# Projecting q two tiles ahead in the windowed-attention layers of a six-layer network

## The chip, the cores and the metric

The kernel runs on one core of one Trainium2 chip. The metric is the time of one execution on the device in microseconds (us). The profile covers one execution of the kernel before; the names of the engines in it are PE (TensorE matmul), PEld (TensorE weight load), DVE (VectorE), ACT (ScalarE), POOL (GpSimd) and SP (SyncE, which issues the DMAs).

## The reference

A sequence of 2048 tokens with 128 features goes through two blocks of pre-normalised attention, a feed-forward part with four-bit quantisation between them, and then six layers of another network. Only these six layers are touched by the change. Each layer is, with 16 heads of 64 elements and windows of 32 tokens:

```python
for i in range(DEPTH):                                # DEPTH = 6
    x = attn_layer(shift_tokens(x), ...) + x
    x = ffn_layer(shift_tokens(x), ...) + x

def attn_layer(x, Wqkv, qs, ksc, Wo):
    q, k, v = jnp.split(x @ Wqkv, 3, -1)              # 3 x 1024 columns, 16 heads
    q = l2norm(q) * qs;  k = l2norm(k) * ksc
    q = q * cos * scale + rotate_half(q) * sin * scale
    k = k * cos / scale + rotate_half(k) * sin / scale
    out = local_attention(q, k, v)                    # softmax over this window and the one before
    return out @ Wo
```

The feed-forward part is a layer norm, two products, a gelu gate and a third product.

## The kernel before, in words

The function `layers` writes, by hand, one instruction list for each engine. The only order within an engine is the one written, and engines meet only through counting semaphores: an instruction that waits holds up all that stands behind it on its engine. Layers 0 to 4 run in a hardware loop, the sixth layer is written out once more behind it. Within a layer the 2048 tokens are 16 tiles of 128 (`NT` = 16). The names below carry (l, T): layer and tile.

For each tile the steps are, with the engine that does them:

- `project(T, i, b)` (PE, L1023): the product of the tile with half of the columns of q (i = 0), k (i = 1) or v (i = 2); b is the half. q and k both go to PSUM banks 0 and 1, so each half waits until the `normalise` of the previous one has read the bank. v goes to the banks of the scores and waits for `subtract` of the tile before. Each half is two matmul rows in the trace.
- `squares` (ACT, L1231), `sum_squares` (DVE, L1376 twice and L1378), `inverse_norms` (ACT, L1237 and L1239), `normalise` (DVE, L1389, two halves): the L2 norm of q and of k.
- `cosines` (DVE, L1397) and `rotate` (POOL, L966 and L967 into the single buffer `sine`) make the two rotary products. For q, POOL adds them too (L973). For k, `add_rotated` on DVE does (L1405).
- `turn(T, r)` (PE, L1037): four transposes; r = 0 and 1 are q, 2 and 3 are k. `store_qk` (ACT, L1252 to L1259) copies the result out.
- `scores` (PE, L1048 and L1055), `maxima` and `subtract` (DVE, L1411 and L1417), `exponentials` (ACT, L1267), `sums` (DVE, L1424 and L1426), `normalise_weights` (POOL, L990): the softmax.
- `turn_weights` (PE, L1070), `place_low` (ACT, L1273) and `place_high` (DVE, L1433): the weights, transposed, each half f in two parts. `values` (PE, L1088), `store_o` (ACT, L1281), `out_project` (PE, L1100) and `residual` (DVE, L1440) finish a tile.

The steps of several tiles are interleaved: in iteration T of `attend`, before the change, each engine works on the norms of q and k of tile T+1, the scores of T, the values of T-1 and the output projection of T-2. SP moves a copy of v, shifted by a window, with two DMAs for each tile. After the 16 tiles comes `forward`, the feed-forward part.

## Time and profile before

| | |
|---|---|
| median of 3 runs | 3716.92 us (3702.21 to 3720.24) |
| the profiled execution: its time, its span | 3709.67 us, 3707.6 us |
| mean granted TensorE clock | 0.926 of full speed |
| busy: PE, PEld, DVE, ACT, POOL | 2984.7, 1623.0, 2847.8, 2071.5, 1071.0 us |
| first and last product of the layers (L1023) | 1647.7 us, 3634.0 us |
| DMA | 100.96 MB, mean 27 GB/s |

The span is the time from the first to the last instruction in the trace. A busy time sums the time in which an engine works on an instruction; waiting is not in it. The clock is a share of TensorE's full 2.4 GHz. The six layers fill the span from 1614 us on.

### The profile page before, as it was taken

What the parts mean: (1) busy time and instruction counts of PE and PEld (TensorE: products, weight loads), DVE (VectorE), ACT (ScalarE), POOL (GpSimd) and SP (SyncE); (2) the same over time, 40 slices, a digit from 0 to 9 for tenths busy, and PEclk for the clock granted to TensorE, in tenths of its full rate; (3) what the DMA queues carried; (4) which work ended last, traced back from release to release, by engine and by line L of the source; (5) the groups of instructions that cost most, each with busy time, mean ns of one, the idle gap of its engine ahead of it and who ended that gap; (6) DMA issues with size and microseconds to landing.
All of it is one profiled execution on the core that took longest, in us unless ns stands there. A gap on an engine that the chain in (4) does not pass through costs nothing. (4 is left out here: it accounts for less than half of the span.)

```text
span 3707.6 us, 73298 instructions
## 1 busy us (share of the span) xinstructions
PE 2984.7 (81%) x28669; PEld 1623.0 (44%) x28669; DVE 2847.8 (77%) x4196; ACT 2071.5 (56%) x3147; POOL 1071.0 (29%) x614
## 2 busy tenths in 40 slices
PE   4999999944369999957887888788878878887888
PEld 1233333313223333325663565466455635654664
DVE  5999999957626778737886887788678868877885
ACT  2577777752213455636664666566556646665664
POOL 0000000000000000035553554455355535544561
PEclk7899999977657898969999999999999999999999
DMA  3000000000120000011111111011111111110110
GB/s 114 29 1 2 2 2 2 1 7 0 64 66 1 2 1 1 1 50 35 34 46 28 30 30 48 25 34 30 36 36 30 45 33 30 30 48 24 36 30 23
DMA packets 57088, 100.96 MB, mean 27 GB/s; under 512 B 20182, under 2 KB 38548, under 8 KB 55316
## 3 DMA queue, kind: packets, MB, share of 16 engines
q1 hardware_dynamic: 56740, 96.18, 8.8%
q8 instruction: 236, 3.87, 0.4%
q14 instruction: 112, 0.92, 0.1%
HBM read 38.22 MB, written 7.34 MB: 12 GB/s over the span
## 5 line engine op out<-in xcount | busy, mean ns | idle before, releaser
L471 DVE TENSOR_REDUCE a_part<-ps 128x1 f32<-128x512 f32 (+3 forms) x1664 | 993.4, 653 | 204.5 <-PE ps L343 190.4
L452 ACT ACTIVATE a_Pb<-ps 128x1024 f32<-128x1024 f32 (+3 forms) x832 | 767.8, 975 | 475.3 <-PE ps L417 472.2
L1023 PE MATMUL ps<-l_w_qkv,l_XS 128*128 128x512 f32 x1152 | 577.5, 624 | 217.5 <-DVE l_weights L1417 158.1
L343 PE MATMUL ps<-a_KS,a_QS 48*128 48x512 bf16 (+3 forms) x1664 | 503.4, 398 | 66.7 <-DMA a_QS<-pieces 30.5
L966 POOL TENSOR_TENSOR l_sine<-l_qn,l_tab 128x512 f32<-128x512 f32 x192 | 341.1, 1777 | 641.9 <-DVE l_qn L1389 641.4
L393 PE MATMUL ps<-a_Pb,V 128*32 128x256 f32 (+2 forms) x6144 | 441.2, 402 | 0.9 <-ACT a_Pb L452 0.9
L1376 DVE TENSOR_REDUCE l_bounded<-l_square 128x8 f32<-128x512 f32 x384 | 254.6, 684 | 217.9 <-ACT l_square L1231 211.9
L1023 PEld LDWEIGHTS ps<-l_w_qkv,l_XS 128*128 128x128 f32 x1152 | 203.7, 197 | 393.4 <-DVE l_weights L1417 170.6
L417 PE MATMUL ps<-a_QS,a_KS 50*128 50x512 bf16 (+3 forms) x1664 | 323.2, 379 | 17.3 <-ACT a_Pb L452 14.9
L1389 DVE TENSOR_TENSOR l_qn<-ps,l_norm 128x512 f32<-128x512 f32 x384 | 246.7, 684 | 86.7 <-ACT l_norm L1239 86.7
L1037 PE MATMUL ps<-ident,l_hat 128*128 128x128 f32 x1536 | 217.8, 276 | 115.2 <-DVE l_hat L1405 115.2
L343 PEld LDWEIGHTS ps<-a_KS,a_QS 48*128 48x128 bf16 x1664 | 125.3, 94 | 422.4 <-DVE a_part L471 322.7
L1037 PEld LDWEIGHTS ps<-ident,l_hat 128*128 128x128 f32 x1536 | 178.8, 141 | 230.6 <-issue 196.1
L990 POOL TENSOR_TENSOR l_weights<-l_weights,l_rcp 128x1024 f32<-128x1024 f32 x96 | 188.9, 1968 | 282.5 <-DVE l_rcp L1426 282.5
L1397 DVE TENSOR_TENSOR l_cosine<-l_qn,l_tab 128x1024 f32<-128x1024 f32 x192 | 252.0, 1312 | 9.4 <-POOL l_tab L981 5.3
L1231 ACT ACTIVATE l_square<-ps 128x512 f32<-128x512 f32 x384 | 228.4, 596 | 42.9 <-PE ps L1023 35.0
L967 POOL TENSOR_TENSOR l_sine<-l_qn,l_tab 128x512 f32<-128x512 f32 x192 | 247.7, 1290 | 0.0
L973 POOL TENSOR_TENSOR l_hat<-l_cosine,l_sine 128x1024 f32<-128x1024 f32 x96 | 226.8, 2363 | 20.5 <-POOL l_sine L967 19.3
L1055 PEld LDWEIGHTS ps<-l_kT,l_qT 128*64 128x64 f32 x6144 | 195.8, 138 | 82.8 <-issue 82.8
L393 PEld LDWEIGHTS ps<-a_Pb,V 128*32 128x32 f32 x6144 | 158.9, 110 | 167.1 <-issue 87.6
L631 POOL MEMSET f_w<- 128x1120 f32 x1 | 1.0, 1032 | 777.7 <-POOLq L284 777.7
L1055 PE MATMUL ps<-l_kT,l_qT 128*64 128x64 f32 x6144 | 222.4, 226 | 0.0
(182 smaller groups left out, 4554.8 us busy)
## 6 DMA issues: line engine op xcount, KB each, us to landing
l_V_earlier<-l_V SPq DMA_DIRECT2D x96, 384.0 KB, 3.5
l_V_earlier<-l_V SPq DMA_DIRECT2D x96, 128.0 KB, 3.4
l_w_qkv<-in_L_ffn_Wqkv_dram SPq DMA_DIRECT2D x6, 1536.0 KB, 8.1
pieces<-a_piece SPq DMA_DIRECT2D x12, 512.0 KB, 2.6
a_QS<-pieces SPq DMA_DIRECT2D x96, 64.0 KB
a_KS<-pieces SPq DMA_DIRECT2D x24, 192.0 KB
l_w_o<-in_L_ffn_Wo_dram SPq DMA_DIRECT2D x6, 512.0 KB, 4.0
a_cos<-in_c_cos_dram SPq DMA_DIRECT2D x2, 1024.0 KB, 5.4
```

The costliest lines, as they stand in the source:

```text
L343: mm = e.matmul(bank[:, 0:width], QS[rows, c, pair, qt * P:(qt + 1) * P], KS[rows, pair, b * CH:b * CH + width], start=not masked, stop=Tr ...
L393: mm = e.matmul(O[32 * h:32 * h + 32, a:b], t.V[:, kt, w:w + 32], Pb[:, n % 2, h, a:b], start=(kt == 0), stop=(kt == tiles_of(c) - 1), ski ...
L417: mm = e.matmul(ps[:, h, a:CH], KS[rows, 2 * g + p, kt * P:(kt + 1) * P], QS[rows, c, 2 * g + p, a:CH], start=not diagonal, stop=True, ski ...
L452: e.activation(Pb[:, n % 2, 2 * p:2 * p + 2, a:CH], ps[:, 2 * p:2 * p + 2, a:CH], ACT.Exp)\
L471: e.tensor_reduce(part[:, u % 2, column(h, qt), b:b + 1], bank[:, 0:width], AX.X, ALU.max)\
L966: e.tensor_tensor(sine[:, :, 0:ROT], swap[:, :, ROT:LD], table[:, :, 0:ROT], ALU.mult).then_inc(s.rotated, 1)
L967: e.tensor_tensor(sine[:, :, ROT:LD], swap[:, :, 0:ROT], table[:, :, ROT:LD], ALU.mult).then_inc(s.rotated, 1)
L1023: e.matmul(ps[:, (V_BANK[T] if i == 2 else 0) + b, :], XS[:, T * P:(T + 1) * P], w_qkv[:, at:at + CH], start=True, stop=True).then_inc(s.a ...
L1037: tr = e.transpose(ps[:, TURN_BANK[r], j * P:(j + 1) * P], hat[:, i, at:at + P], t.ident[:, :])
L1055: mm = e.matmul(ps[half:half + LD, bank, at:at + LD], qT[:, T % 2, j, w, :, :], kT[:, T % 2, j, WIN * w:WIN * (w + 2)], start=False, stop= ...
L1376: e.tensor_reduce(bounded[:, heads, 0], square[:, heads, :], AX.X, ALU.add).then_inc(s.total, 1)
L1397: e.tensor_tensor(cosine[:, i, :, :], qn[:, i, :, :], tab[:, 2 * i, T, :].unsqueeze(1).to_broadcast([P, LH, LD]), ALU.mult).then_inc(s.cos ...
```

## The change

Order and placing are changed in the layers' attention part; no arithmetic is.

- q is projected two tiles ahead. In iteration T, `project(T + 2, 0, .)` stands behind `values(T - 1)` and ahead of the projection of v, where q of T+1 was projected between the turns of T, behind v. `squares`, `sum_squares`, `inverse_norms`, `normalise` and `cosines` of q move with it on ACT and DVE, `rotate` of q on POOL is renamed but keeps its place. At T = 0 the q of tile 1 is done by itself.
- k of T+1 is projected ahead of `turn_weights(T - 1)`, where it was behind it.
- The turns 0 and 1 of q follow each other, and `out_project` stands between turn 1 and turn 2 as before.
- `add_rotated` moves from behind the sums to ahead of them, and one tile earlier: in iteration T it adds k of T+1.
- ACT: the k squares stand ahead of `place_low`, and `inverse_norms` of k between its two halves. DVE: `place_high`'s halves stand ahead of and behind `normalise` of k.
- v's products count on a semaphore of their own (`v_ready`), and the clearing of 32 old semaphores gets a block of its own ahead of the layers' first one.

```diff
--- before.py
+++ after.py
@@ -860,6 +860,12 @@
...
+        with nc.Block() as block:
+            @block.sync
+            def _(e):
+                for signal in t.spent:
+                    e.sem_clear(signal)
...
-                    for signal in t.spent:
-                        e.sem_clear(signal)
@@ -909,7 +913,7 @@
                 def load_weights(l):
-                    e.wait_ge(s.a_ready, START + l * (6 * NT))
+                    e.wait_ge(s.v_ready, START + l * (2 * NT))
                     e.dma_start(w_qkv[:, :], a["L1_ffn_Wqkv"][l]).then_inc(s.w_qkv, 16)
@@ -991,11 +995,13 @@
                 def attend(l):
+                    rotate(l, 1, 0)
                     for T in range(NT):
                         if T + 1 < NT:
-                            for i in range(2):
-                                rotate(l, T + 1, i)
+                            rotate(l, T + 1, 1)
                         normalise_weights(l, T)
+                        if T + 2 < NT:
+                            rotate(l, T + 2, 0)
 
...
+                e.sem_inc(s.v_ready, START)
@@ -1021,7 +1028,7 @@
                     e.matmul(ps[:, (V_BANK[T] if i == 2 else 0) + b, :], XS[:, T * P:(T + 1) * P], w_qkv[:, at:at + CH],
-                             start=True, stop=True).then_inc(s.a_ready, 1)
+                             start=True, stop=True).then_inc(s.v_ready if i == 2 else s.a_ready, 1)
 
@@ -1118,27 +1125,29 @@
                         ahead = T + 1 < NT
-                        if ahead:
-                            project(l, T + 1, 0, 0)
+                        if T == 0:
+                            project(l, 1, 0, 0)
+                            project(l, 1, 0, 1)
                         turn(l, T, 0)
-                        if ahead:
-                            project(l, T + 1, 0, 1)
                         turn(l, T, 1)
                         if T >= 2:
                             out_project(l, T - 2)
                         turn(l, T, 2)
                         turn(l, T, 3)
+                        if ahead:
+                            project(l, T + 1, 1, 0)
+                            project(l, T + 1, 1, 1)
                         if T:
                             turn_weights(l, T - 1, 0)
                             turn_weights(l, T - 1, 1)
-                        if ahead:
-                            project(l, T + 1, 1, 0)
-                            project(l, T + 1, 1, 1)
                         scores(l, T, 0)
                         scores(l, T, 1)
                         if T:
                             values(l, T - 1, 0)
                             values(l, T - 1, 1)
+                        if T + 2 < NT:
+                            project(l, T + 2, 0, 0)
+                            project(l, T + 2, 0, 1)
                         if ahead:
@@ -1225,7 +1234,7 @@
                     n = (l * NT + T) * 2 + i
-                    e.wait_ge(s.a_ready, START + (l * NT + T) * 6 + 2 * i + b + 1)
+                    e.wait_ge(s.a_ready, START + (l * NT + T) * 4 + 2 * i + b + 1)
                     if b == 0:
@@ -1239,7 +1248,7 @@
                 def store_values(l, T):
-                    e.wait_ge(s.a_ready, START + (l * NT + T) * 6 + 6)
+                    e.wait_ge(s.v_ready, START + (l * NT + T) * 2 + 2)
                     e.copy(V[:, T % 3, :], flat2(ps[:, V_BANK[T]:V_BANK[T] + 2, :])).then_inc(s.v_done, 1)
@@ -1295,27 +1304,30 @@
                         ahead = T + 1 < NT
-                        if ahead:
-                            squares(l, T + 1, 0, 0)
-                        store_qk(l, T, 0)
-                        if ahead:
-                            squares(l, T + 1, 0, 1)
-                        store_qk(l, T, 1)
-                        if ahead:
-                            inverse_norms(l, T + 1, 0)
-                        store_qk(l, T, 2)
-                        store_qk(l, T, 3)
-                        if T:
-                            place_low(l, T - 1, 0)
-                            place_low(l, T - 1, 1)
+                        if T == 0:
+                            squares(l, 1, 0, 0)
+                            squares(l, 1, 0, 1)
+                            inverse_norms(l, 1, 0)
+                        for r in range(4):
+                            store_qk(l, T, r)
                         if ahead:
                             squares(l, T + 1, 1, 0)
                             squares(l, T + 1, 1, 1)
+                        if T:
+                            place_low(l, T - 1, 0)
+                        if ahead:
                             inverse_norms(l, T + 1, 1)
+                        if T:
+                            place_low(l, T - 1, 1)
                         if T:
                             store_o(l, T - 1, 0)
                             store_o(l, T - 1, 1)
+                        if T + 2 < NT:
+                            squares(l, T + 2, 0, 0)
+                            squares(l, T + 2, 0, 1)
                         exponentials(l, T)
+                        if T + 2 < NT:
+                            inverse_norms(l, T + 2, 0)
                         if ahead:
@@ -1456,32 +1468,35 @@
                         ahead = T + 1 < NT
-                        if T:
-                            sums(l, T - 1)
-                        if ahead:
-                            sum_squares(l, T + 1, 0)
-                        if T:
-                            add_rotated(l, T)
-                        if ahead:
-                            normalise(l, T + 1, 0)
-                            cosines(l, T + 1, 0)
+                        if T == 0:
+                            sum_squares(l, 1, 0)
+                            normalise(l, 1, 0)
+                            cosines(l, 1, 0)
                         if T >= 2:
                             residual(l, T - 2)
                         if not ahead:
                             e.wait_ge(s.added, START + l * NT + NT - 2)
                             for c in range(NC - 1):
                                 shift(c, s.xs)
+                        if ahead:
+                            sum_squares(l, T + 1, 1)
                         if T:
                             place_high(l, T - 1, 0)
+                        if ahead:
+                            normalise(l, T + 1, 1)
+                        if T:
                             place_high(l, T - 1, 1)
-                        if ahead:
-                            sum_squares(l, T + 1, 1)
-                            normalise(l, T + 1, 1)
                         maxima(l, T)
                         subtract(l, T)
+                        if T + 2 < NT:
+                            sum_squares(l, T + 2, 0)
                         if ahead:
                             cosines(l, T + 1, 1)
-                    sums(l, NT - 1)
+                            add_rotated(l, T + 1)
+                        sums(l, T)
+                        if T + 2 < NT:
+                            normalise(l, T + 2, 0)
+                            cosines(l, T + 2, 0)
                     residual(l, NT - 2)
```

VectorE, from the maxima of one tile on (inside the loop over the layers; `l_bounded` and `l_norm` are sum_squares, `l_qn` normalise, `l_hat` add_rotated, `l_total` and `l_rcp` sums, `X` the residual). Before:

```order
L1411 TENSOR_REDUCE l_nmax<-ps 128x16
L1417 TENSOR_TENSOR l_weights<-ps,l_nmax 128x1024
L1397 TENSOR_TENSOR l_cosine<-l_qn,l_tab 128x1024
L1424 TENSOR_REDUCE l_total<-l_weights 128x16
L1426 RECIPROCAL l_rcp<-l_total 128x16
L1376 TENSOR_REDUCE l_bounded<-l_square 128x8
L1378 TENSOR_REDUCE l_norm<-l_bounded 128x16
L1405 TENSOR_TENSOR l_hat<-l_cosine,l_sine 128x1024
L1389 TENSOR_TENSOR l_qn<-ps,l_norm 128x512 x2
```

And now:

```order
L1423 TENSOR_REDUCE l_nmax<-ps 128x16
L1429 TENSOR_TENSOR l_weights<-ps,l_nmax 128x1024
L1388 TENSOR_REDUCE l_bounded<-l_square 128x8
L1390 TENSOR_REDUCE l_norm<-l_bounded 128x16
L1409 TENSOR_TENSOR l_cosine<-l_qn,l_tab 128x1024
L1417 TENSOR_TENSOR l_hat<-l_cosine,l_sine 128x1024
L1436 TENSOR_REDUCE l_total<-l_weights 128x16
L1438 RECIPROCAL l_rcp<-l_total 128x16
L1401 TENSOR_TENSOR l_qn<-ps,l_norm 128x512 x2
```

The norms of q (now of T+2) come ahead of k's cosines and addition, and the sums behind both; in both lists q's cosines (not shown) follow the last row.

TensorE, from the last values product of a tile to the output projection (`l_hat` are the turns, `l_oT` the output projection). Before:

```order
L1088 MATMUL ps<-l_wT,l_V 64x2x32 x2
L1023 MATMUL ps<-l_w_qkv,l_XS 128x512 x2
L1019 ISA
L1023 MATMUL ps<-l_w_qkv,l_XS 128x512
L1037 MATMUL ps<-ident,l_hat 128x128 x4
L1100 MATMUL ps<-l_oT,l_w_o 128x128 x8
```

And now:

```order
L1095 MATMUL ps<-l_wT,l_V 64x2x32 x2
L1026 ISA
L1030 MATMUL ps<-l_w_qkv,l_XS 128x512 x4
L1044 MATMUL ps<-ident,l_hat 128x128 x4
L1107 MATMUL ps<-l_oT,l_w_o 128x128 x8
```

The four products in a row are q of T+2 and then v of T+1; before, v stood first and q's two halves stood around the first turn.

## Rows read from the trace of the kernel before

**Rows 1.** Busy time by stretch: us, each engine's busy time, granted clock, DMA share.
```profile
2026.81:2045.92 19.11, 13.57 (x140) 8.81 (x142) 14.42 (x21) 10.16 (x19) 10.17 (x6) 0.91 0.23 56
2045.92:2274.84 228.92, 190.39 (x2378) 138.07 (x2376) 188.92 (x261) 146.28 (x274) 132.67 (x78) 1.00 0.11 31
```

**Rows 2.** VectorE's timeline, one tile: start, us, operation, idle before it and releaser.
```profile
1757.46 1.22 DVE L1411 TENSOR_REDUCE l_nmax<-ps 128x16 f32<-128x1024 f32 x1
1758.71 1.23 DVE L1417 TENSOR_TENSOR l_weights<-ps,l_nmax 128x1024 f32<-128x1024 f32 x1
1759.85 1.42 DVE L1397 TENSOR_TENSOR l_cosine<-l_qn,l_tab 128x1024 f32<-128x1024 f32 x1
1761.19 1.21 DVE L1424 TENSOR_REDUCE l_total<-l_weights 128x16 f32<-128x1024 f32 x1
1762.43 0.25 DVE L1426 RECIPROCAL l_rcp<-l_total 128x16 f32<-128x16 f32 x1
1763.59 0.69 DVE L1376 TENSOR_REDUCE l_bounded<-l_square 128x8 f32<-128x512 f32 x1 [0.91 <-ACT l_square L1231]
1765.27 0.69 DVE L1376 TENSOR_REDUCE l_bounded<-l_square 128x8 f32<-128x512 f32 x1 [0.99 <-ACT l_square L1231]
1765.99 0.19 DVE L1378 TENSOR_REDUCE l_norm<-l_bounded 128x16 f32<-128x32 f32 x1
1766.29 1.23 DVE L1405 TENSOR_TENSOR l_hat<-l_cosine,l_sine 128x1024 f32<-128x1024 f32 x1
1767.44 1.28 DVE L1389 TENSOR_TENSOR l_qn<-ps,l_norm 128x512 f32<-128x512 f32 x2
1768.75 1.23 DVE L1397 TENSOR_TENSOR l_cosine<-l_qn,l_tab 128x1024 f32<-128x1024 f32 x1
1769.89 0.28 DVE L1440 TENSOR_TENSOR X<-X,ps 128x128 f32<-128x128 f32 x1
1770.21 1.30 DVE L1433 COPY l_wT<-ps 64x512 f32<-64x512 f32 x2
1771.54 1.28 DVE L1376 TENSOR_REDUCE l_bounded<-l_square 128x8 f32<-128x512 f32 x2
...
1773.87 1.29 DVE L1389 TENSOR_TENSOR l_qn<-ps,l_norm 128x512 f32<-128x512 f32 x2 [0.82 <-ACT l_norm L1239]
1775.07 1.22 DVE L1411 TENSOR_REDUCE l_nmax<-ps 128x16 f32<-128x1024 f32 x1
```

**Rows 3.** TensorE's timeline in the same tile.
```profile
1759.99 2.84 PE L1023 MATMUL ps<-l_w_qkv,l_XS 128*128 128x512 f32 x6 [1.67 <-DVE l_weights L1417]
...
1767.65 1.09 PE L1037 MATMUL ps<-ident,l_hat 128*128 128x128 f32 x8 [1.30 <-DVE l_hat L1405]
...
1769.48 1.88 PE L1023 MATMUL ps<-l_w_qkv,l_XS 128*128 128x512 f32 x4
1771.20 0.38 PE L1048 MATMUL ps<-l_mask_c,identb 128*128 128x512 bf16 x1
...
1772.59 0.39 PE L1048 MATMUL ps<-l_mask_c,identb 128*128 128x512 bf16 x1
```

**Rows 4.** ScalarE's timeline in the same tile.
```profile
1759.97 1.06 ACT L1267 ACTIVATE l_weights<-l_weights 128x1024 f32<-128x1024 f32 x1 [1.02 <-DVE l_weights L1417]
...
1762.01 1.01 ACT L1243 COPY l_V<-ps 128x1024 f32<-128x1024 f32 x1 [0.98 <-PE ps L1023]
...
1762.96 0.60 ACT L1231 ACTIVATE l_square<-ps 128x512 f32<-128x512 f32 x1
```

**Rows 5.** GpSimd's timeline in the same tile.
```profile
1762.77 1.90 POOL L990 TENSOR_TENSOR l_weights<-l_weights,l_rcp 128x1024 f32<-128x1024 f32 x1 [2.58 <-DVE l_rcp L1426]
...
1768.88 2.22 POOL L966 TENSOR_TENSOR l_sine<-l_qn,l_tab 128x512 f32<-128x512 f32 x1 [4.22 <-DVE l_qn L1389]
```

**Rows 6.** Timeline at the first layer's start, GpSimd.
```profile
1660.35 1.25 POOL L966 TENSOR_TENSOR l_sine<-l_qn,l_tab 128x512 f32<-128x512 f32 x1
1661.56 2.24 POOL L967 TENSOR_TENSOR l_sine<-l_qn,l_tab 128x512 f32<-128x512 f32 x1
```

**Rows 7.** Timeline at the same moment, VectorE.
```profile
1660.38 2.30 DVE L1397 TENSOR_TENSOR l_cosine<-l_qn,l_tab 128x1024 f32<-128x1024 f32 x1 [5.33 <-POOL l_tab L981]
```

**Rows 8.** TensorE's timeline at the start of the second layer.
```profile
2019.43 3.78 PE L1023 MATMUL ps<-l_w_qkv,l_XS 128*128 128x512 f32 x4 [3.59 <-DVE l_qn L1389]
```

**Rows 9.** VectorE's timeline where the layers' first block begins.
```profile
1614.79 2.29 DVE L38 TENSOR_REDUCE stat<-x 128x16 f32<-128x2048 f32 x1 [0.38 <-PEq L284]
```

More of the change, by code:

```diff
@@ L815, in layers @@
     with ExitStack() as ctx:
-        s = semaphores(ctx, nc, "l_", "w_qkv w_tab w_o w_mlp xs tab a_ready square total root qn cosine v_done rotated "
+        s = semaphores(ctx, nc, "l_", "w_qkv w_tab w_o w_mlp xs tab a_ready v_ready square total root qn cosine v_done rotated "
                        "t_ready t_free s_ready nmax sub exp_done sums rcp normed p_ready low high earlier_even earlier_odd "
```

## The prediction

> **What bounds the kernel now.** I read the busy time by stretch first. In thirteen consecutive tiles of the second layer (from one `maxima` to the fourteenth) the clock is full, and VectorE is busy for 188.92 and TensorE for 190.39 of 228.92 us [rows 1]. A tile takes 228.92 / 13 = 17.61 us, and neither engine is full: two engines near 14.6 us each wait for each other. So the timeline of one tile is what counts, VectorE's first. It shows three waits: 0.91 and 0.99 us for the squares of q and 0.82 us for the inverse norms of k, 2.72 us in all [rows 2]. The other 14.9 us are work, from start to start.
>
> Why are q's squares late? On TensorE v's products wait for `subtract` (1.67 us idle), and q's stand behind v's in the queue [rows 3]. The v copy runs on ScalarE at 1762.01 and the first square only at 1762.96 [rows 4]; the second stands behind a store of turned q. So the chain is subtract, v, q, squares, sum_squares, then k's addition, for which TensorE idles another 1.30 us [rows 3]. It is a loop through both engines, once per tile.
>
> **The change part by part.** No instruction is added to a tile or removed. I lay out one tile anew, with t = 0 at the start of `maxima(T)`, service times from start to start and the latencies of the rows.
>
> Service times on VectorE [rows 2]: maxima 1.25, subtract 1.14, sums 1.24, one half of sum_squares 0.72, bound 0.30, add_rotated 1.15, normalise 1.31 (1.20 where a step without dependence follows), cosines 1.14, residual 0.32, one half of place_high 0.67. Cosines of k take 1.34 now; 0.2 of that is the port wait below. TensorE: half a projection 0.86 (k's two halves start at 1769.48, the mask product at 1771.20), q's or k's turns and turn_weights about 0.9 each, one half of the scores 1.40 [rows 3]. One half of values is 0.93: scores end at 1773.99, that is 1756.38 a tile earlier, and the modelled end of values is 1759.99 - 1.67 = 1758.32. Latencies: TensorE to ScalarE 0.30 (v's four rows end at 61.71, the copy starts at 62.01), ScalarE to VectorE 0.03 to 0.14, VectorE to TensorE 0.12.
>
> *q two tiles ahead.* `place_high` of the second half ends at t = 0, values' second half takes 0.1 to 1.03, q's halves end at 1.89 and 2.75, its squares at 2.79 and 3.65. VectorE has finished maxima and subtract at 2.39, so it waits 0.43, and 0.14 before the second half. Two waits of 1.90 become 0.57. v's products (2.75 to 4.47) no longer wait: subtract ended at 2.5. What is behind them now, turns of q and the output projection, runs to 7.2.
>
> *Addition ahead of the sums.* VectorE goes on: bound from 4.40, k's cosines 4.70, add_rotated 5.84, sums 6.98, reciprocal 8.22, normalise q 8.50. The exponentials (1.06 [rows 4]) stand behind q's squares on ScalarE and end at 4.7, so the sums find them. k's turns start at 7.2, without a wait, where 1.30 stood. GpSimd makes k's sines right after `normalise` of k, by about 3, long before 5.84.
>
> *k ahead of turn_weights.* TensorE now has a wait here: k's first half needs q's first half read, at 9.3, and the turns end at 8.1. This idle 1.2 us has turn_weights, scores and values queued behind it. k's products end at 11.02, turn_weights at 11.9, scores at 14.7. VectorE needs the scores only at 16.3, so this costs nothing; its cover is 1.4 us.
>
> *The port.* The sums are later, so `normalise_weights` on GpSimd (1.90 [rows 5]) runs from 8.56 to 10.46, and q's cosines are ready at 9.81. The trace shows what happens when GpSimd and a VectorE instruction with two inputs from SBUF meet: at 1660.38 cosines took 2.30 instead of 1.23, waiting for the end of L966, and L967, issued meanwhile, took 2.24 instead of about 1.25, waiting for the cosines [rows 6, 7]. A 2.22 us sine behind q's cosines is the same on the other side [rows 5]. They exclude each other for a whole instruction. So q's cosines start at 10.46: 0.65 us of new waiting; between 0 (no overlap) and 1.9 (the whole instruction) I take what the layout gives. In return k's cosines meet nobody, and the 0.2 goes.
>
> *The rest of the tile.* Residual 11.60, k's sums of squares 11.92 (squares ready at 11.1 and 11.9), bound 13.36, first half of place_high 13.58, which covers most of the former 0.82 wait; inverse norms are ready at 14.38 (0.13 idle), normalise k to 15.58, second half to 16.27, `maxima(T+1)` at 16.28. ScalarE's longer block is the v copy (5.3 to 6.3), then the stores; the turn in bank 2 waits for the first store until 7.55, just before it is due.
>
> Sum per tile: 17.61 - 1.33 (q's squares) - 0.69 (inverse norms) + 0.65 (port) - 0.2 + about 0.25 of dispatch and seams = 16.3. The gain is 1.31 us, with 13 such intervals in each of 6 layers: 78 x 1.31 = 102 us. The sixth layer is not in the loop; I take the same gain there.
>
> *First interval of a layer*: 19.11 us [rows 1]. Laid out in the same way, without values and place_high, it gives 15.5, so 6 x 3.6 = 22 us. *Last interval*: residual and shifts of X are also behind the later `normalise_weights`; the shifts are SBUF copies and wait for the port. About +0.4, or 2 us in all. *Head of a layer*: at T = 0 all stores stand behind q's inverse norms on ScalarE, which costs, but k's products no longer start 3.59 us idle and at the low clock (3.78 us for four rows against 1.88 [rows 8, 3]). I get 2.2 us less before the first `maxima`; bounds are +3 (the stores come last) and -4; 6 x 2 = 12 us. *The extra block*: the boundary before the layers cost VectorE 0.38 us [rows 9]; one more of those and 32 clears that nothing hides any longer: between 0.4 and 5, I take 3 us.
>
> Total: 102 + 22 - 2 + 12 - 3 = 131 us off the profiled execution's 3709.7. The median of the runs lies 7 us above it, so 3717 - 131, rounded to **3585 us**.
>
> **The rivals.** A measurement of this kernel can tell about 0.5%, 19 us, from no change.
>
> 1. *The seams are smaller or the port collision misses.* If q's cosines come just before or after normalise_weights, a tile takes 15.65; 78 x 0.65 = 51 us more: 3534. For it: the collision depends on an overlap of 0.65 us. Against: normalise q depends on nothing that could move it by that much.
> 2. *A second small wait remains.* The layout has narrow places: the turn in bank 2 (slack 0.1), the squares of k (0.0), ScalarE's queue before the stores. One of them late by 0.7 us per tile: 16.95, or 55 us less gained: 3640.
> 3. *Slower: GpSimd keeps the port.* Behind normalise_weights, GpSimd has q's two sines ready at 9.94. If its queue went on ahead of the waiting cosines, they would start at 10.46 + 2 x 1.26 = 12.98. That is 2.5 us per tile, on the path of everything that follows: 18.8 us per tile, +1.2 x 78 = 94, less 29 of the other terms: 3782. It decides from 1.3 us of extra wait on. The one meeting in the trace in which GpSimd had its next instruction ready speaks against it: the cosines came after one instruction, and L967 waited [rows 6, 7]. The Trainium skill (SBUF - State Buffer, "Who interferes with whom") says that whoever issues first has the pair of ports for its whole instruction; by that, too, the cosines, issued before the sines, would go first, and the sum would stay at 3585.
> 4. *No gain: the loop closes elsewhere.* The slack of 1.4 us before the scores may be eaten, if k's addition or q's normalise moves by more than that; then the tile is bound by TensorE (14.65 us of work and 1.2 idle, plus new waits) near 17.6, and only the ends of the layers gain: about 3690 to 3715.
>
> That the change does not do what it says can be left out: the orders of both engines show it.
>
> **How the numbers follow.** The forecast itself (3560 to 3615) has 0.60, rival 1 has 0.14, rival 2 has 0.14, rival 3 has 0.06, rival 4 has 0.06, two thirds of it within 0.5%. So faster 0.90, same 0.04, slower 0.06. The range takes the forecast with rivals 1 and 2 at their own times: 3530 to 3645.
>
> **What the profile would show.** Right: `maxima` every 16.3 us; two waits for squares of q under 0.5 us each; no idle on TensorE before v's products or k's turns, but 1.2 us before k's products; q's cosines at about 1.75 us and k's at 1.23; normalise_weights still 1.90. Rival 1: cosines 1.23 both. Rival 2: a wait on VectorE above 0.5 us for squares, or on TensorE for a store. Rival 3: q's cosines above 3 us. Rival 4: VectorE waiting for TensorE's scores before `maxima`. I would be wrong altogether if the tile stayed at 17.6 with the waits moved.

## The result and the profile after

The change makes the kernel faster: 3596.97 us, the median of 4 runs (3591.6 to 3605.64), against 3714.53 us for the kernel before on the same chip (4 runs, 3702.21 to 3720.24). The ratio is 0.969, with a 95% interval of 0.9657 to 0.9723. The profiled execution has a span of 3591.1 us, 116.5 less than before, and took 3592.9 us.

The stretches of the second layer first, from the first `maxima` to the second, and the thirteen tiles that follow (columns as in [rows 1]):

```profile
2009.39:2024.52 15.13, 11.97 (x134) 7.58 (x132) 14.63 (x20) 10.49 (x20) 9.50 (x6) 1.00 0.28 71
2024.52:2235.34 210.82, 193.00 (x2366) 140.90 (x2366) 195.33 (x261) 147.01 (x274) 132.83 (x79) 1.00 0.12 34
```

A tile takes 210.82 / 13 = 16.22 us where it took 17.61 [rows 1] (16.20 in twelve of thirteen intervals); VectorE is busy for 93% of it (83% before), TensorE for 92%, at the full clock in both. The time came out of waiting. VectorE's timeline of one tile, from one `maxima` to the next, answers to [rows 2]:

```profile
2137.95 1.23 DVE L1423 TENSOR_REDUCE l_nmax<-ps 128x16 f32<-128x1024 f32 x1
2139.21 1.22 DVE L1429 TENSOR_TENSOR l_weights<-ps,l_nmax 128x1024 f32<-128x1024 f32 x1
2141.03 1.45 DVE L1388 TENSOR_REDUCE l_bounded<-l_square 128x8 f32<-128x512 f32 x2 [0.59 <-ACT l_square L1240]
2142.52 0.19 DVE L1390 TENSOR_REDUCE l_norm<-l_bounded 128x16 f32<-128x32 f32 x1
2142.62 1.22 DVE L1409 TENSOR_TENSOR l_cosine<-l_qn,l_tab 128x1024 f32<-128x1024 f32 x1
2143.97 1.23 DVE L1417 TENSOR_TENSOR l_hat<-l_cosine,l_sine 128x1024 f32<-128x1024 f32 x1
2145.12 1.21 DVE L1436 TENSOR_REDUCE l_total<-l_weights 128x16 f32<-128x1024 f32 x1
2146.36 0.25 DVE L1438 RECIPROCAL l_rcp<-l_total 128x16 f32<-128x16 f32 x1
2146.53 1.24 DVE L1401 TENSOR_TENSOR l_qn<-ps,l_norm 128x512 f32<-128x512 f32 x2
2147.81 1.87 DVE L1409 TENSOR_TENSOR l_cosine<-l_qn,l_tab 128x1024 f32<-128x1024 f32 x1
2149.60 0.28 DVE L1452 TENSOR_TENSOR X<-X,ps 128x128 f32<-128x128 f32 x1
2149.80 1.27 DVE L1388 TENSOR_REDUCE l_bounded<-l_square 128x8 f32<-128x512 f32 x2
2151.10 0.19 DVE L1390 TENSOR_REDUCE l_norm<-l_bounded 128x16 f32<-128x32 f32 x1
2151.32 0.69 DVE L1445 COPY l_wT<-ps 64x512 f32<-64x512 f32 x1
2152.11 1.29 DVE L1401 TENSOR_TENSOR l_qn<-ps,l_norm 128x512 f32<-128x512 f32 x2
2153.43 0.69 DVE L1445 COPY l_wT<-ps 64x512 f32<-64x512 f32 x1
2154.16 1.23 DVE L1423 TENSOR_REDUCE l_nmax<-ps 128x16 f32<-128x1024 f32 x1
```

Of the three waits for other engines one is left as such, 0.59 us for q's squares (0.91 and 0.99 before); the second half of the squares is in the 1.45 us of the merged row, where two reductions without a wait take 1.27 (2149.80). Of the 0.82 us for k's inverse norms 0.10 is left (`place_high` ends at 2152.01, `normalise` starts at 2152.11); the first half of `place_high` covers the rest. New is the length of q's cosines: 1.87 us at 2147.81, where 1.23 stood.

TensorE in the same tile, to be read against [rows 3]:

```profile
2139.15 3.70 PE L1030 MATMUL ps<-l_w_qkv,l_XS 128*128 128x512 f32 x8
2142.68 1.04 PE L1044 MATMUL ps<-ident,l_hat 128*128 128x128 f32 x8
2143.56 1.95 PE L1107 MATMUL ps<-l_oT,l_w_o 128*128 128x128 f32 x16
2145.34 1.07 PE L1044 MATMUL ps<-ident,l_hat 128*128 128x128 f32 x8
2147.23 1.98 PE L1030 MATMUL ps<-l_w_qkv,l_XS 128*128 128x512 f32 x4 [0.82 <-DVE l_qn L1401]
2149.05 1.04 PE L1077 MATMUL ps<-ident,l_weights 128*128 128x128 f32 x8
```

q's and v's eight rows follow each other without a wait, and so do k's turns (2145.34). The one idle time in these rows is 0.82 us before k's products, for q's `normalise`. GpSimd shows the other side of the long cosines, against [rows 5]:

```profile
2146.70 1.90 POOL L994 TENSOR_TENSOR l_weights<-l_weights,l_rcp 128x1024 f32<-128x1024 f32 x1 [5.67 <-DVE l_rcp L1438]
2148.55 2.26 POOL L970 TENSOR_TENSOR l_sine<-l_qn,l_tab 128x512 f32<-128x512 f32 x1
```

`normalise_weights` runs to 2148.60, the cosines issued at 2147.81 end at 2149.68, 1.08 after that, and the sine issued at 2148.55 takes 2.26 us instead of 1.27.

Where the 116.5 us of span went, by the starts of `maxima` (96 in each trace, six layers):

| stretch | before | after | difference |
|---|---|---|---|
| up to the second attention stage's last division (stages not changed) | 1609.54 | 1614.13 | +4.6 |
| from there to the first `maxima` | 74.29 | 74.31 | 0.0 |
| first to second `maxima` of a layer, 6 of them | 115.94 | 90.69 | -25.3 |
| second to fifteenth, 78 intervals | 1369.11 | 1263.23 | -105.9 |
| fifteenth to sixteenth, 6 | 73.03 | 76.99 | +4.0 |
| sixteenth to the next layer's first, 5 | 400.05 | 406.43 | +6.4 |
| last `maxima` to the end | 65.64 | 65.36 | -0.3 |

### The profile page after: what moved, and what is told of

It reads as the page before. It is cut to its first block and busy times, and to the rows that moved or that the text cites. A ratio compares the mean times of both kernels' runs of the same rounds, so it can differ in the third digit from the quotient of the medians.

```text
span 3591.1 us, 72940 instructions
## 1 busy us (share of the span) xinstructions
PE 3005.4 (84%) x28669; PEld 1639.0 (46%) x28669; DVE 2894.9 (81%) x4196; ACT 2076.7 (58%) x3147; POOL 1061.8 (30%) x614
## 5 line engine op out<-in xcount | busy, mean ns | idle before, releaser
L1030 PE MATMUL ps<-l_w_qkv,l_XS 128*128 128x512 f32 x1152 | 565.4, 625 | 127.9 <-DVE l_qn L1401 86.8
L1409 DVE TENSOR_TENSOR l_cosine<-l_qn,l_tab 128x1024 f32<-128x1024 f32 x192 | 292.3, 1523 | 9.6 <-POOL l_tab L985 5.5
L1290 ACT COPY l_oT<-ps 128x512 f32<-128x512 f32 x192 | 112.3, 585 | 226.8 <-PE ps L1095 226.8
L1095 PE MATMUL ps<-l_wT,l_V_earlier 128*64 128x64 f32 x3072 | 193.2, 224 | 46.6 <-DVE l_wT L1445 44.2
L1044 PE MATMUL ps<-ident,l_hat 128*128 128x128 f32 x1536 | 204.7, 277 | 23.3 <-ACT l_qT L1262 17.1
```

Of the source, the lines that this page charges most:

```text
L1030: e.matmul(ps[:, (V_BANK[T] if i == 2 else 0) + b, :], XS[:, T * P:(T + 1) * P], w_qkv[:, at:at + CH], start=True, stop=True).then_inc(s.v ...
L1409: e.tensor_tensor(cosine[:, i, :, :], qn[:, i, :, :], tab[:, 2 * i, T, :].unsqueeze(1).to_broadcast([P, LH, LD]), ALU.mult).then_inc(s.cos ...
```

## The experiments

All are edits of the changed kernel. The medians of two of them come from different chips unless said, and in these traces the unchanged stages ahead of the layers end up to 33 us apart. So I judge by the tile, the distance of two `maxima` in layers 0 to 4 (the value that most of the 65 have), and give the median beside it.

### q behind v again

```diff
+                        if ahead:
+                            project(l, T + 1, 2, 0)
+                            project(l, T + 1, 2, 1)
                         if T + 2 < NT:
                             project(l, T + 2, 0, 0)
                             project(l, T + 2, 0, 1)
-                        if ahead:
-                            project(l, T + 1, 2, 0)
-                            project(l, T + 1, 2, 1)
```

> The changed kernel with v's products put back ahead of q's on TensorE; all else stays as changed. Theory: the gain comes from q's squares no longer standing behind v, which waits for subtract. With v first, the products of q start 1.7 us after subtract instead of right behind values; the squares come about 3.1 us later, and VectorE, with k's cosines, the addition and the sums now queued behind q's sums of squares, has nothing to cover it. One tile takes 19.0 to 19.4 us instead of 16.20, the wait for q's squares is above 3 us, the time is about 3597 + 78 x 3.0 = 3830 us (3790 to 3860). Rival (the gain is in the order on VectorE): the tile stays below 17 us and the time below 3660.

Measured: 3955.84 us (3951.21 to 3966.6), ratio to the kernel before 1.065 (1.0614 to 1.0687); a tile takes 20.46 us. So this order carries the gain, and without it the rest of the change is a loss. But the tile is 1.1 to 1.5 us longer than I expected. VectorE's wait for q's squares, and TensorE in that tile:

```profile
2223.12 1.45 DVE L1388 TENSOR_REDUCE l_bounded<-l_square 128x8 f32<-128x512 f32 x2 [3.65 <-ACT l_square L1240]
```

```profile
2219.52 3.70 PE L1030 MATMUL ps<-l_w_qkv,l_XS 128*128 128x512 f32 x8 [1.27 <-DVE l_weights L1429]
...
2227.41 1.09 PE L1044 MATMUL ps<-ident,l_hat 128*128 128x128 f32 x8 [1.53 <-DVE l_hat L1417]
2229.32 3.68 PE L1030 MATMUL ps<-l_w_qkv,l_XS 128*128 128x512 f32 x4 [0.81 <-DVE l_qn L1401]
```

The wait is 3.65 us; that was forecast. What was not is the last row: k's four rows take 3.68 us instead of 1.98. Over this tile the mean granted clock is 0.92 of full, where it was 1.00: TensorE was idle for 1.27, 1.53 and 0.81 us in this tile up to k's products, and with the clock at its lower level of 1.2 GHz these products take 1.7 us longer. That this is what makes the tile longer than expected can be read from the same trace. 64 of its 65 tiles have a mean clock of 0.92; the one at full clock, in the first layer, takes 19.26 us, within the forecast, and k's products in it take 1.99 us:

```profile
1713.19:1732.45 19.26, 15.61 (x213) 11.48 (x208) 15.02 (x20) 11.65 (x22) 8.91 (x6) 1.00 0.10 29
```

### The sums ahead of k's addition again

```diff
                             cosines(l, T + 1, 1)
-                            add_rotated(l, T + 1)
                         sums(l, T)
+                        if ahead:
+                            add_rotated(l, T + 1)
```

> The changed kernel with the softmax sums put back ahead of k's addition on VectorE. Theory: the order of these two is worth next to nothing. k's turns come 1.3 us later and take up the idle time that TensorE has before k's products (0.8 us), and q's cosines meet normalise_weights all the same, since that now waits for the addition's port first. A tile takes 16.2 to 16.5 us, the time is 3595 to 3620. Rival (the addition ahead of the sums carries part of the gain, 1.1 us per tile): 17.3 us per tile, 3680 us.

Measured: 3574.58 us (3572.21 to 3575.77), ratio 0.9619 (0.9591 to 0.9647); a tile takes 15.96 us. Undoing this part is a gain of 0.24 us per tile. The rival is out, and so is my "next to nothing" by its sign. VectorE's addition and q's cosines, and `normalise_weights` on GpSimd:

```profile
2146.64 1.23 DVE L1417 TENSOR_TENSOR l_hat<-l_cosine,l_sine 128x1024 f32<-128x1024 f32 x1
...
2149.09 1.61 DVE L1409 TENSOR_TENSOR l_cosine<-l_qn,l_tab 128x1024 f32<-128x1024 f32 x1
```

```profile
2146.66 2.96 POOL L994 TENSOR_TENSOR l_weights<-l_weights,l_rcp 128x1024 f32<-128x1024 f32 x1 [4.36 <-DVE l_rcp L1438]
```

The addition gets the port first and `normalise_weights`, issued 0.02 us behind it, takes 2.96 us. It ends at 2149.62, 0.53 us after q's cosines are issued (2149.09), instead of 0.79 us after: they take 1.61 us instead of 1.87. That is about the 0.24. The later turns of k cost TensorE an idle time (1.16 us before them) in place of the one before k's products.

### k behind turn_weights again

```diff
-                        if ahead:
-                            project(l, T + 1, 1, 0)
-                            project(l, T + 1, 1, 1)
                         if T:
                             turn_weights(l, T - 1, 0)
                             turn_weights(l, T - 1, 1)
+                        if ahead:
+                            project(l, T + 1, 1, 0)
+                            project(l, T + 1, 1, 1)
```

> The changed kernel with k's products put back behind turn_weights on TensorE. Theory: turn_weights now waits for normalise_weights, which ends about 10.4 us into the tile; k's products behind it start at 11.4 instead of 9.3, and k's squares, needed by VectorE at 11.9, come at 13.2 and 14.0. A tile takes 17.7 to 18.2 us, all of the change's gain per tile is gone, the time is about 3597 + 78 x 1.7 = 3730 us (3710 to 3755). Rival (TensorE has slack, the order there does not matter): 16.2 to 16.5 us and below 3620.

Measured: 3821.82 us (3813.72 to 3824.13), ratio 1.0289 (1.0259 to 1.0319). The tile is not one number: 31 of the 65 tiles take 18.0 to 18.2 us at full clock, and the other 34 take 19.3 to 19.7 us at a mean clock of 0.91, in changing order. Two tiles in a row, TensorE and the granted clock:

```profile
2149.28 1.39 PE L1077 MATMUL ps<-ident,l_weights 128*128 128x128 f32 x8 [2.31 <-POOL l_weights L994]
2150.46 3.31 PE L1030 MATMUL ps<-l_w_qkv,l_XS 128*128 128x512 f32 x4
...
2168.99 1.09 PE L1077 MATMUL ps<-ident,l_weights 128*128 128x128 f32 x8 [2.31 <-POOL l_weights L994]
2169.92 1.88 PE L1030 MATMUL ps<-l_w_qkv,l_XS 128*128 128x512 f32 x4
```

```profile
2138.51:2158.22 19.71, 16.34 (x181) 11.52 (x182) 15.21 (x21) 11.28 (x21) 10.18 (x7) 0.91 0.10 28
2158.22:2176.24 18.02, 14.72 (x181) 10.84 (x182) 15.20 (x20) 11.37 (x21) 10.18 (x7) 1.00 0.11 31
```

Both have the same wait of 2.31 us for `normalise_weights`. In the tile of 18.02 us, within my bounds, k's products take 1.88 us at clock 1.00; in the tile of 19.71 us they take 3.31 us, at a mean clock of 0.91. So this part of the change is needed too (1.8 us per tile), and its absence costs the clock on top in 34 of 65 tiles. The Trainium skill (TensorE: Matmul & The Clock Gate, "Part 1: The HAM clock gate") describes such a gate, which knows two levels and lets the full clock through only behind recent activity; the two forms of one tile, at 1.00 and 0.91, agree with that.

### Half of normalise_weights

```diff
-                    e.tensor_tensor(weights[:, T % 2, :, :], weights[:, T % 2, :, :],
-                                    rcp[:, :].unsqueeze(2).to_broadcast([P, LH, LD]), ALU.mult).then_inc(s.normed, 1)
+                    e.tensor_tensor(weights[:, T % 2, 0:HALF, :], weights[:, T % 2, 0:HALF, :],
+                                    rcp[:, 0:HALF].unsqueeze(2).to_broadcast([P, HALF, LD]), ALU.mult).then_inc(s.normed, 1)
```

> normalise_weights multiplies only the first 8 of 16 heads; the other 8 heads' weights stay without the division by their sums. Theory of the port: GpSimd is done before q's cosines are issued, so these fall from 1.87 to 1.23 us and a tile from 16.20 to 15.5 to 15.7 us; the time is 3597 - 78 x 0.6 = 3550 us (3540 to 3560). Rival (the cosines are longer for another reason, or the time comes back as a wait elsewhere): cosines 1.87 or the tile at 16.2, 3590 to 3600 us.

This kernel leaves out the division for half of the heads; it serves only to measure. Measured: 3548.07 us (3538.77 to 3553.47), ratio 0.9541 (0.9511 to 0.9572); a tile takes 15.71 us. `normalise_weights` and then q's cosines:

```profile
2143.93 1.04 POOL L994 TENSOR_TENSOR l_weights<-l_weights,l_rcp 128x512 f32<-128x512 f32 x1 [5.82 <-DVE l_rcp L1438]
```

```profile
2145.04 1.23 DVE L1409 TENSOR_TENSOR l_cosine<-l_qn,l_tab 128x1024 f32<-128x1024 f32 x1
```

GpSimd is done at 2144.97, the cosines are issued at 2145.04 and take 1.23 us. The port theory holds, and the gain lies within what I expected: 0.49 us of the tile for 0.64 us of port wait (0.15 us comes back at k's squares, whose two reductions take 1.42 instead of 1.27 us).

### The residual in the port's wait

```diff
                             normalise(l, T + 2, 0)
+                            if T:
+                                residual(l, T - 1)
                             cosines(l, T + 2, 0)
```

The residual at its old place remains for the last tiles.

> The changed kernel with the residual of T-1 between normalise q and q's cosines. Theory of the port: normalise_weights holds the port until 0.64 us after q's cosines are issued. The residual reads one operand from PSUM, so it can run in that time (0.28 us) and comes for free. Cosines 1.5 to 1.6 instead of 1.87, a tile 15.85 to 15.95, 3597 - 78 x 0.3 = 3574 us. Rival (cosines are long by themselves, or the residual waits for the port too): 1.87 or a residual of 0.9, a tile at 16.2 and 3590 to 3605.

Measured: 3582.73 us (3571.44 to 3607.66), ratio 0.965 (0.9625 to 0.9675); a tile takes 16.00 us, 0.2 less.

```profile
2141.84 0.28 DVE L1452 TENSOR_TENSOR X<-X,ps 128x128 f32<-128x128 f32 x1
2142.03 1.79 DVE L1409 TENSOR_TENSOR l_cosine<-l_qn,l_tab 128x1024 f32<-128x1024 f32 x1
```

The residual, with one operand in PSUM, is not held up (0.28 us). The cosines still take 1.79 us, not 1.5 to 1.6. They are issued 1.35 us behind the start of `normalise` instead of 1.28, since `normalise` hands over to the residual sooner than to the dependent cosines, so only 0.08 us of their wait is gone; what is gained is that the residual no longer stands behind them. The direction is right, but the tile gains 0.2 us where I expected about 0.3. The median cannot tell it from the change as it stands; the tile can.

### Both halves of place_high ahead of normalise k

```diff
                         if T:
                             place_high(l, T - 1, 0)
+                            place_high(l, T - 1, 1)
                         if ahead:
                             normalise(l, T + 1, 1)
-                        if T:
-                            place_high(l, T - 1, 1)
```

> The changed kernel with both halves of place_high ahead of normalise k on VectorE. Theory: what is left of a tile beyond VectorE's work are 0.59 us of waiting for q's squares, about 0.1 us for k's inverse norms and 0.64 us for the port. The squares wait for values' second half, and that for place_high's. With place_high earlier, values, q's products and the squares come about 0.55 us earlier, and the 0.1 is covered. A tile takes 15.5 to 15.7 us, 3597 - 78 x 0.6 = 3550 us. Rival (q's products then wait for normalise k to read their bank, and nothing is gained): 16.1 to 16.3 us, 3590 to 3605.

Measured: 3537.51 us (3534.62 to 3538.9), ratio 0.9538 (0.9521 to 0.9554); a tile takes 15.44 us, 0.76 less, a little more than expected. The sums of squares of q begin nearly without a wait:

```profile
2145.09 1.45 DVE L1388 TENSOR_REDUCE l_bounded<-l_square 128x8 f32<-128x512 f32 x2
```

### Both of these, and with the sums first

> place_high ahead of normalise k and the residual ahead of q's cosines together. Theory: TensorE now limits as well, since k's products start when normalise q's first half is done, and from there to the next squares of q there are 9.1 us of TensorE work and handover; with 6.2 us from these squares to k's products that makes 15.3. So 15.3 to 15.5 us, 3597 - 78 x 0.8 = 3535 us. Rival (both gains add up on VectorE alone): 15.2 or less, 3520.

> The same two edits with the sums ahead of k's addition. The sums first gave 15.96 us instead of 16.20 for a tile, against my expectation, because normalise_weights starts earlier relative to q's cosines. Here the later turns of k count: k's products start 6.55 us behind q's squares instead of 6.2, and with 9.1 us back to the squares TensorE's loop gives 15.6 us. Theory: 15.5 to 15.7 us, so about 3597 - 78 x 0.6 = 3550 us, slower than e3_both. Rival (VectorE is the only limit): 15.1 us, 3512 us, faster than e3_both.

Measured on the chip of the two runs before: 3533.95 us (3525.48 to 3553.56), ratio 0.9531 (0.9514 to 0.9548), for both, and 3556.32 us (3545.33 to 3571.03), ratio 0.9585 (0.9548 to 0.9622), with the sums first. The tiles are 15.44 and 15.69 us. With both edits a tile is as long as with place_high alone, and what the residual saved stands as a wait for q's squares:

```profile
2144.31 1.45 DVE L1388 TENSOR_REDUCE l_bounded<-l_square 128x8 f32<-128x512 f32 x2 [0.35 <-ACT l_square L1240]
```

So VectorE is no longer what limits; the loop through TensorE is. The sums first, worth 0.24 us before, now cost 0.25, as the loop says. The rivals of both are out.

### q's products between the two halves of values

```diff
                         if T:
                             values(l, T - 1, 0)
-                            values(l, T - 1, 1)
                         if T + 2 < NT:
                             project(l, T + 2, 0, 0)
                             project(l, T + 2, 0, 1)
+                        if T:
+                            values(l, T - 1, 1)
```

This is made on top of both edits, and on ScalarE q's squares go between the two store_o in the same way.

> e3_both with q's products between the two halves of values on TensorE, and q's squares between the two store_o on ScalarE. Theory: 15.44 us per tile in e1_highs and e3_both alike is TensorE's loop (k's products, turn_weights, scores, both values, q's product, squares). Moving 0.9 us of values out of it frees VectorE of the 0.35 us of waiting for q's squares, and its own work with the rest of the port wait gives 15.05 to 15.15 us per tile: 3534 - 78 x 0.33 = 3508 us (3500 to 3520). Rival (something else than the second half of values holds the squares): 15.4 and 3530.

Measured: 3492.88 us (3489.05 to 3504.22), ratio 0.9409 (0.9391 to 0.9426); a tile takes 14.84 us, 0.6 less and 0.2 better than the best I expected, and the median lies below my 3500 to 3520. VectorE's cosines and sums of squares of q:

```profile
2122.01 1.79 DVE L1411 TENSOR_TENSOR l_cosine<-l_qn,l_tab 128x1024 f32<-128x1024 f32 x1
...
2130.17 1.27 DVE L1390 TENSOR_REDUCE l_bounded<-l_square 128x8 f32<-128x512 f32 x2
```

The two reductions take 1.27 us, without a wait ahead of them or between them. By these rows the expectation counted only the 0.35 us ahead of the squares and left out the wait between them (1.45 against 1.27 us): 15.44 - 0.35 - 0.18 = 14.91. VectorE's work, from start to start, is now the tile, with 0.5 us of port wait in it.

> e10_qmid with the sums ahead of k's addition. With TensorE's loop 0.9 us shorter, k's products may start at 6.55 instead of 6.2 us behind q's squares without being the limit (6.55 + 8.15 = 14.7), so VectorE alone counts, and there the sums first were worth 0.25 us as long as the cosines met normalise_weights. Theory: 14.85 to 15.0 us, about 3495 us, the fastest. Rival (the loop still counts, as in e9_sums_both, which lost 0.25): 15.3 or more.

Measured: 3488.66 us (3482.71 to 3493.33), ratio 0.9389 (0.9374 to 0.9404); nearly all tiles take 14.78 to 14.88 us. The loop no longer counts, so the rival is out, but nothing is won either, where I had called it the fastest: the cosines take 1.53 instead of 1.79 us, and the addition makes up for it with its later hand-over. The two orders are level.

### The head of a layer

```diff
                         for r in range(4):
+                            if T == 0 and r < 2:
+                                squares(l, 1, 0, r)
+                            if T == 0 and r == 2:
+                                inverse_norms(l, 1, 0)
                             store_qk(l, T, r)
```

TensorE has the second product of q between the turns 0 and 1 again, for T = 0 alone.

> The changed kernel with the first tile of each layer in the old interleaving: q's second product between the turns 0 and 1, its squares between the stores, the inverse norms behind the second store. This is the term of the sum that came out wrong: I had put the head of a layer at 2.2 us less than before, and it is 0.5 us more. Theory: waiting for q's inverse norms ahead of the stores costs TensorE its second pair of turns and its clock; with the old order the stretch from the last shift to the first maxima goes from 15.41 to 14.5 to 15.0 us, the tile stays at 16.20, and the time falls by 2 to 6 us, below what a median can tell. Rival (the head is set by the feed-forward part's end): 15.4 us.

Measured: 3595.24 us (3584.92 to 3598.09), ratio 0.967 (0.9651 to 0.969): no difference that a median could tell, as expected. In the second layer the stretch from the last shift to the first `maxima` is 13.24 us. TensorE in that stretch as changed, with the stretch's row, and k's products and the stretch in this experiment:

```profile
1994.21 3.01 PE L1030 MATMUL ps<-l_w_qkv,l_XS 128*128 128x512 f32 x4 [2.87 <-DVE l_XS L1460]
...
2001.73 1.05 PE L1044 MATMUL ps<-ident,l_hat 128*128 128x128 f32 x4 [2.54 <-ACT l_qT L1262]
2002.57 3.22 PE L1030 MATMUL ps<-l_w_qkv,l_XS 128*128 128x512 f32 x4
```

```profile
1993.98:2009.39 15.41, 12.20 (x91) 7.42 (x92) 7.96 (x12) 8.60 (x16) 5.80 (x3) 0.78 0.11 32
```

```profile
2009.12 1.98 PE L1030 MATMUL ps<-l_w_qkv,l_XS 128*128 128x512 f32 x4 [2.14 <-DVE l_qn L1402]
```

```profile
2001.47:2014.71 13.24, 10.27 (x90) 6.48 (x92) 7.97 (x13) 8.60 (x16) 4.64 (x3) 0.87 0.13 37
```

As changed, the turn waits 2.54 us for a store that stands behind the inverse norms, and k's products then take 3.22 us, at a mean clock of 0.78. In the old interleaving that wait is gone and the products take 1.98 us at 0.87. The gain is more than the 0.4 to 0.9 us expected, here. The same stretch differs from layer to layer, though: 15.41, 15.00, 15.30, 15.46 and 13.57 us as changed, 13.24, 14.60, 15.07, 13.20 and 13.68 us here, so 1.0 per layer. From the sixteenth `maxima` to the next layer's first, summed over five layers, it is 406.43 - 400.17 = 6.3 us, of which the first intervals give back 1.4 (92.10 instead of 90.68 us for six).

> e10_qmid and e8_head together. Theory: the head's gain adds to e10_qmid as it stands: same 15.1 us per tile, 0.5 to 1 us less in the head of each layer, 3503 us. Rival: no difference from e10_qmid in the head.

Measured: 3487.24 us (3481.04 to 3490.36), ratio 0.9386 (0.9371 to 0.94), on the chip of e10_qmid and e12_qmid_sums; tiles of 14.84 us, the tile of e10_qmid and not the 15.1 us expected, and the five ends take 396.14 us against 402.73: 1.3 per layer where I expected 0.5 to 1, and the rival is out. This is the best version, level with e12_qmid_sums: 227 us below the kernel before (3713.93 us on that chip), and 108 below the 3595.24 us of e8_head on the same chip, which has the tile of the change.

## Why the prediction was right

Its number, 3585 us, lies 12 us (0.3%) under the median, inside the range. The mechanism of the gain per tile is the one that was laid out; one of the smaller terms, the head of a layer, was wrong. Of the 131 us forecast off the profiled execution 116.5 came. Against their forecasts the terms gave 3.9 us more (tiles), 3.3 more (first intervals), 3 more (extra block), 2.0 less (last intervals) and 18.4 less (heads); another 4.6 less is a difference in stages that the change does not touch.

- *The tile.* Forecast 16.3 us, measured 16.20. The gain of the 78 intervals was put at 102 us and is 105.9; the sixth layer, for which the same gain was taken, gave 1.17 us per interval against 1.39 in the loop. That q's place ahead of v carries it is shown: with q behind v the tile is 20.46. That the tile came out to 0.1 us is in part luck. Against its rows, the layout has 2.82 us from `maxima` to q's squares (3.08 measured), 1.14 from k's cosines to the addition (1.35: the 1.14 was read where a step without dependence follows), 0.30 for the bound (0.10), 0.28 from the reciprocal to `normalise` (0.17), 0.32 for the residual (0.20) and 1.44 for k's squares (1.30). These errors nearly cancel.
- *q's squares.* Forecast 0.43 and 0.14 us of remaining wait, measured 0.59 and 0.18. That the first half of place_high covers k's inverse norms is read from the rows of one tile; no run undoes that part alone.
- *The port.* Forecast 0.65 us at q's cosines, measured 1.87 - 1.23 = 0.64. Halving normalise_weights took all of it away. Rival 3 is out: in all 84 tiles in which q's cosines met normalise_weights, GpSimd started its next sine without an idle time of its own, and the waiting cosines went first (1.6 to 1.9 us, and none of all 192 above 2.30). But the prediction's reason against it, "the one meeting in the trace in which GpSimd had its next instruction ready", overlooked a meeting of other instructions in the same trace, shown under *The extra block* below, in which VectorE had to wait for two of GpSimd. That trace did not rule rival 3 out.
- *k's products.* Forecast 1.2 us of idle ahead of them, measured 0.82, and covered as said. "Its cover is 1.4 us" was not put to the test by the change; with k behind turn_weights the wait outgrows it.
- *The addition.* The prediction counted this part for the wait that it removes before k's turns. It does remove it, but that wait would have cost nothing in the new order, and the part costs 0.24 us per tile, since it lets q's cosines meet normalise_weights for longer. This holds for this order of the rest: on top of both edits the addition first gains 0.25, and with q between the halves of values the two are level.
- *First and last interval of a layer.* Forecast -22 and +2 us, measured -25.3 and +4.0.
- *The head of a layer.* This term was wrong, in size and sign: "I get 2.2 us less before the first maxima", 12 us in all. Measured from the sixteenth `maxima` to the next layer's first it is +6.4 us for five layers, 1.3 each, 0.4 of it in all ahead of the head, in the feed-forward part. The step that failed is "k's products no longer start 3.59 us idle and at the low clock": in the second layer the 3.59 us of idle before them are gone, but the turn ahead of them waits 2.54 us for a store behind q's inverse norms, and they still take 3.22 us; q's products take 3.01 us for four rows there, where they took 1.12 and 1.02 us before, a loss that the sum had no term for. With the old interleaving back the ends of the layers take 400.17 us, as before the change (400.05). This term accounts for 18 us too much gain, more than the 12 us of the miss.
- *The extra block.* Forecast 3 us. VectorE's first instruction of the layers, against [rows 9], came 2.5 us later behind its predecessor:

```profile
1621.89 2.29 DVE L38 TENSOR_REDUCE stat<-x 128x16 f32<-128x2048 f32 x1 [2.88 <-PEq L863]
```

The stretch from the attention stage to the first `maxima` is equal all the same (74.29 and 74.31 us). 2.17 of the 2.5 us come back at VectorE's next instruction, a TENSOR_SCALAR of 128x16 that takes 5.10 us before and 2.93 us after. (The same operation at L46 takes 0.17 us in both traces.) GpSimd's memsets run beside it. Before, with the second memset that it waited for:

```profile
1617.11 5.10 DVE L40 TENSOR_SCALAR stat<-stat 128x16 f32<-128x16 f32 x1
1619.95 2.23 POOL L879 MEMSET l_kT<- 128x2560 f32 x1
```

And after, with the same memset, for which it did not wait:

```profile
1624.21 2.93 DVE L40 TENSOR_SCALAR stat<-stat 128x16 f32<-128x16 f32 x1
1627.05 2.26 POOL L883 MEMSET l_kT<- 128x2560 f32 x1
```

In both traces it is issued 0.6 us behind the start of the memset of `qT`. Before, it ends with the second memset (1622.21 and 1622.18); after, it ends with the first (1627.14, where `kT`'s begins). In each of the twelve other traces with the extra block it takes 2.93 us. That the memsets held it up is read from these ends alone. The second memset started 2.84 us after the TENSOR_SCALAR was issued, so the prediction's rule that whoever issues first goes first does not account for it; why GpSimd kept its turn is open, and no run has the change without the block. So the 3 us forecast for the block are about right for the boundary itself, and that they did not show in the time is luck: this shorter wait took most of them back.

## What to carry to other kernels

Where two engines are each 80% busy and wait for each other once per tile, lay out one tile with measured start-to-start times: the layout gave 16.3 for 16.20 us, with errors of 0.1 to 0.3 us that nearly cancelled. Look for the product that stands, in an in-order queue, behind one that waits for something it does not need, and move it ahead; after each such move ask again which engine closes the loop, since the same reordering (sums first) gained 0.24, lost 0.25 and changed nothing in three surroundings. Price a new wait on TensorE with the slower products that may follow it, not at its own length alone: 2.31 us of waiting brought 1.3 to 1.7 us more in half of the tiles here.

## What the runs showed of the hardware

- TensorE's clock falls inside a steady loop, too. With 2.31 us of idle before turn_weights in a tile of 18 us, k's four rows took 1.88 us in one tile and 3.31 in another, at 1.00 and 0.91 of mean granted clock; with 3.6 us of idle in three pieces it happened in 64 of 65 tiles. The loss, 1.4 to 1.7 us, came on top of the wait. The kernel before, idle for 1.67 and 1.30 us in its tile, ran its thirteen tiles at 1.00.
- In these traces VectorE and GpSimd excluded each other for whole instructions when VectorE read two operands from SBUF, and the one issued first went first, by as little as 0.02 us: the addition at 2146.64 held up normalise_weights, issued at 2146.66, by 1.06 us. The longest of the 192 cosines in the trace took 2.30 us, so none of them waited for more than one GpSimd instruction. A VectorE instruction with one tensor operand in SBUF, the TENSOR_SCALAR of L40, seems to have been held up by memsets too: by one in the trace of the change (2.93 us), by two in the trace before (5.10 us). If so, a waiting VectorE instruction does not always come next.
